# Attention maxima of a group placed by a table of ticks, on both sides of the value visits

## The reference

```
mod = silu(c) @ wmod                      # six parts of 1024 for each of the 4 batches
h = layernorm(x) * (1 + ca) + sa
q, k, v = h @ Wq, h @ Wk, h @ Wv          # 32 query heads, 8 key/value heads, 32 wide
q, k = rope(q), rope(k)
att = where(causal, q @ k.T / sqrt(32), -inf)
ctx = softmax(att) @ v                    # 1024 queries x 1024 keys for each head
x = x + ga * (ctx @ Wo)
h = layernorm(x) * (1 + cb) + sb
out = x + gb * (h @ W.T + bias + lora(h))
```

## Time and profile before

| | |
|---|---|
| median of three runs | 2497.97 us |
| the profiled execution | 2495.66 us, of it the span 2493.9 us |
| PE, DVE, ACT, POOL busy | 97%, 69%, 42%, 66% of the span |
| granted TensorE clock | 0.99 (mean) |
| last part of the chain, PE L1586 and L1539 | 14% and 13% of the span |

### The profile page before, as it was taken

The page is one execution under the profiler, slowest core; times in us unless marked ns, Lnnn a source line. Parts: engine busy times, 40 slices in busy tenths (PEclk is TensorE's granted clock), DMA queues, the critical chain, the costliest instruction groups (busy, mean ns, idle before and its releaser), DMA issues. The chain is left out here.

```text
span 2493.9 us, 36376 instructions
## 1 busy us (share of the span) xinstructions
PE 2406.7 (97%) x13140; PEld 1668.3 (67%) x13204; DVE 1723.4 (69%) x3392; ACT 1042.6 (42%) x1873; POOL 1650.8 (66%) x865
## 2 busy tenths in 40 slices
PE   5999999999999999999999999998999999999998
PEld 3788888887555555555555555544788788888886
DVE  4866666677888888888888888874555355455553
ACT  3433333231666666666666666665211111111111
POOL 3744333441799998999989999993655455545643
PEclk8999999999999999999999999999999999999999
DMA  6532333352545325344233345313333333323330
GB/s 236 198 118 87 115 113 118 123 150 80 162 100 146 82 64 154 83 132 97 71 79 83 83 117 132 84 31 127 112 92 101 103 90 97 118 86 104 107 93 25
DMA packets 179727, 267.45 MB, mean 107 GB/s; under 512 B 20508, under 2 KB 113884, under 8 KB 178400
## 3 DMA queue, kind: packets, MB, share of 16 engines
q1 hardware_dynamic: 179552, 265.13, 36.2%
HBM read 183.22 MB, written 80.81 MB: 106 GB/s over the span
## 5 line engine op out<-in xcount | busy, mean ns | idle before, releaser
L1082 POOL TENSOR_TENSOR p_sum<-p_sum,p_ring 128x1024 f32<-128x1024 f32 (+2 forms) x465 | 991.3, 2164 | 71.0 <-PE ctx_ps L1143 50.2
L976 ACT ACTIVATE p_ring<-scores 128x512 f32<-128x512 f32 (+1 forms) x896 | 448.9, 568 | 236.3 <-DVE scores L1030 173.6
L272 DVE TENSOR_REDUCE neg_max<-scores_q 128x1 f32<-128x512 f32 x679 | 438.8, 684 | 79.0 <-PE scores_q L253 64.9
L253 PE MATMUL scores_q<-k_stack,q_stack 96*128 96x512 f32 (+1 forms) x1473 | 443.0, 378 | 14.6 <-DVE neg_max L269 6.3
L1122 PE MATMUL scores<-q_stack,k_stack 98*128 98x512 f32 (+1 forms) x1216 | 409.7, 414 | 10.6 <-ACT p_ring L976 7.7
L253 PEld LDWEIGHTS scores_q<-k_stack,q_stack 96*128 96x128 f32 x1473 | 263.6, 191 | 135.4 <-DVE neg_max L269 64.5
L1122 PEld LDWEIGHTS scores<-q_stack,k_stack 98*128 98x128 f32 x1216 | 205.9, 190 | 184.7 <-ACT p_ring L976 71.9
L627 POOL TENSOR_TENSOR roped_hilo<-roped_hilo 128x512 fp32r<-128x512 f32 x80 | 105.5, 1319 | 337.0 <-ACT roped_hilo L467 337.0
L269 DVE CUSTOM_DVE_ANT_0 scores_q<-scores_q,masks 128x512 f32<-128x512 f32 x489 | 296.0, 642 | 38.4 <-PE scores_q L253 38.4
L676 PE MATMUL proj_ps<-h_hi,w_hi 128*128 128x512 f32 x752 | 298.7, 397 | 0.7 <-POOL w_lo L616 0.7
L676 PE MATMUL proj_ps<-h_hi,w_lo 128*128 128x512 f32 x752 | 294.1, 391 | 0.0
(11 more groups left out here) (182 smaller groups left out, 3632.8 us busy)
## 6 DMA issues: line engine op xcount, KB each, us to landing
q_stack<-qk_t SPq DMA_DIRECT2D x96, 512.0 KB, 6.8
qk_t<-roped_hilo SPq DMA_DIRECT2D x80, 512.0 KB, 2.8
x_in<-in_L_attn_resid SPq DMA_DIRECT2D x32, 512.0 KB, 6.3
ctx_t<-ctx_raw SPq DMA_DIRECT2D x64, 256.0 KB, 5.4
prefetched<-in_L_wmod SPq DMA_DIRECT2D x4, 4096.0 KB, 13.6
prefetched<-ctx_t SPq DMA_DIRECT2D x31, 512.0 KB, 4.0
prefetched<-inv_t SPq DMA_DIRECT2D x124, 128.0 KB, 5.5
k_stack<-qk_t SPq DMA_DIRECT2D x96, 128.0 KB, 8.8
```

Of the source, the lines that this page charges most:

```text
L253: last = nc.tensor.matmul(dst[:, a, :], qs[0:MHI, h, i * P:(i + 1) * P], ks[0:MHI, lo:lo + w], start=not first and (a == 0 or not diag), s ...
L272: nc.vector.tensor_reduce(neg, src, AX.X, ALU.max, negate=True).then_inc(sh.s_mx.sem, 1)
L976: nc.scalar.activation(p[:, a * per:(a + 1) * per, :], src[:, a * per:(a + 1) * per, :], ACT.Exp, scale=SM_SCALE).then_inc(s_ex.sem, 1)
L1082: nc.gpsimd.tensor_tensor(a, a, probs(n, u), ALU.add).then_inc(s_ap.sem, 1)
```

## The change

A number with ' is a unit of the group after the next. The code:

```diff
-BATCH = 2
-LAG = 2
-SUM_AT = {1: 9, 0: 16}
-AHEAD = 5
-TURN_AT = 17
-MAX_TICK = [m * NE // NM - AHEAD for m in range(NM)]
+AFTER = [
+    [],
+    maxima(1, 10, 11) + quads(-1, 10, 11) + maxima(1, 12),
+    maxima(1, 13),
+    ...
+    maxima(2, 6, 7, 8) + quads(0, 8, 9) + maxima(2, 9),
+]
+EARLY = [s[2] for r in AFTER for s in r if s[0] == "max" and s[1] == 2]
...
-        for at, t in ((n + 1, u), (n + 2, u - NE)):
-            if at < NG:
-                steps += [("max", at, m) for m in range(NM) if MAX_TICK[m] == t]
...
+        for step in AFTER[u]:
+            at = n + step[1]
+            if 0 <= at < NG and not (step[0] == "sum" and n >= NG - 1):
+                steps.append((step[0], at) + step[2:])
+        if n >= NG - 1:
+            for hf in range(2):
+                if u == SUM_AT_LAST[hf] and 0 <= n - hf < NG:
+                    steps.append(("sum", n - hf, hf))
...
-FIRST_MAXIMA = [(0, m) for m in range(NM)] + [(1, m) for m in range(NM) if MAX_TICK[m] < 0]
+FIRST_MAXIMA = [(0, m) for m in range(NM)] + [(1, m) for m in EARLY]
```

More of the change, by code:

```diff
@@ L99, with maxima, quads, sums_of @@
 QUARTER = D // 4
-MAX_TICK = [m * NE // NM - AHEAD for m in range(NM)]
+def maxima(ahead, *units):
+    return [("max", ahead, m) for m in units]
+def quads(ahead, *quads):
+    return [("values", ahead, q) for q in quads]
+def sums_of(ahead, hf):
+    return [("sum", ahead, hf)]
+def turned(ahead):
+    return [("turn", ahead)]
+AFTER = [
+    [],
+    maxima(1, 10, 11) + quads(-1, 10, 11) + maxima(1, 12),
+    maxima(1, 13),
+    maxima(1, 14, 15),
+    maxima(1, 16),
+    maxima(1, 17) + quads(0, 0, 1) + maxima(1, 18, 19),
+    [],
+    maxima(1, 20, 21, 22) + quads(0, 2, 3) + maxima(1, 23, 24),
+    maxima(1, 25),
+    maxima(1, 26) + sums_of(-1, 1) + maxima(1, 27),
+    [],
+    maxima(1, 28, 29, 30) + quads(0, 4, 5) + maxima(1, 31),
+    maxima(1, 32),
+    maxima(1, 33, 34),
+    maxima(1, 35, 36),
+    maxima(1, 37) + quads(0, 6, 7) + maxima(2, 0, 1),
+    maxima(2, 2) + sums_of(0, 0) + maxima(2, 3),
+    maxima(2, 4) + turned(1) + maxima(2, 5),
+    [],
+    maxima(2, 6, 7, 8) + quads(0, 8, 9) + maxima(2, 9),
+]
+EARLY = [s[2] for r in AFTER for s in r if s[0] == "max" and s[1] == 2]
 def group_steps(n):
@@ L129, in group_steps @@
                 steps.append(({MOD_AT: "mod", MOD_OUT: "mod_out", MOD_IN: "mod_in"}[u], i))
-        at, v = (n, u - LAG) if u >= LAG else (n - 1, u - LAG + NE)
-        if 0 <= at < NG and v == QUADS[QUAD_OF[v]][-1] and QUAD_OF[v] % BATCH == BATCH - 1:
-            steps += [("values", at, q) for q in range(QUAD_OF[v] - BATCH + 1, QUAD_OF[v] + 1)]
     return steps
 STEPS = [s for n in range(NG + 1) for s in group_steps(n)]
-FIRST_MAXIMA = [(0, m) for m in range(NM)] + [(1, m) for m in range(NM) if MAX_TICK[m] < 0]
+FIRST_MAXIMA = [(0, m) for m in range(NM)] + [(1, m) for m in EARLY]
 UNIT_AT = {}
```

## The result

| | before | after |
|---|---|---|
| median (four runs each) | 2497.69 us (2494.40 to 2500.48) | 2458.02 us (2457.52 to 2460.31) |
| ratio, with its 95% interval | 1 | 0.984 [0.983, 0.986] |
| profiled execution, of it the span | 2495.66, 2493.9 us | 2458.49, 2456.7 us |
| plain period of a group | 33.50 us | 31.89 us |

The change makes the kernel 39.7 us faster. The forecast was 2468, with a range of 2456 to 2496. The time lies inside the range, but within 1 us of the first rival, "POOL lags and costs nothing yet" (2459), and outside the forecast's own range of 2461 to 2476.

What follows compares the result with a forecast made beforehand. PE and DVE bound the kernel in turn; DVE's 28.80 us busy plus 3.4 idle made 32.2, so POOL's 32.47 would take over. Thirty periods by 1.0 us: 2497.97 - 30 = 2468 us, range 2456 to 2496.

Steps and rivals of the forecast that it cites:

- POOL lags and costs nothing yet: Rival, attention: POOL falls back 0.3 us a period within its 4.1 us margin, PE's pace counts; 2459 us, chance 0.13.
- The gain taken from DVE's idle times, piece by piece: Attention's plain period: DVE's six idle times shrink from 4.70 to 3.4 us, giving 32.2 us with 28.80 busy.
- POOL takes over, 32.5: Main case, plain groups: POOL's additions become the bound, period 32.5 us, 1.0 less; 2468 us, chance 0.50.
- the forecast's own sign, a period below 32.2: Test in the profile after: the forecast is wrong if the period is above 33.0 or below 32.2 us.
- Occupancy: Skill's rule, rival of no change: busiest engine POOL, 31.97 of 33.50 us, already bounds; 2498 us, chance 0.07.
- The wait of 1.03 us of POOL at tick 11 is gone: Sign at tick 11's visit: POOL's wait gone or below 0.1 us; if still there, POOL is not the bound.
- The turned rows: Turn's DMAs before tick 0's scores: most of the 0.5 us margin goes, costing 0 to 0.6 us, taken as 0.1.
- the slower rival: At the turn: its copy slips, DMAs land late, tick 0's scores wait; 0.3 us a period, 2507 us, chance 0.13.
- The sign that I had set, more than 0.62 us: Wait for the turned rows: if longer than 0.62 us and naming the DMA, the slower case came in part.
- Scores behind the visits cost nothing: Scores stand 0.23 us later behind six visits and two sums; ACT's idle time hides it, at most 1.8 us a period.
- Half of the gain (2483): Rival: ticks 6, 10 and 18 without maxima starve DVE; half the gain, 15 us, is left; chance 0.17.
- Groups with modulation: Attention groups with a piece of modulation, 36.74 us long, should lose the same 1.0 us as plain groups.

Runs made afterwards that it cites:

- after_relief: Changed kernel, with score unit 18's exponentials summed by PE instead of added by POOL, only in groups 25 to 30: 2444.92 us, ratio 0.979.
- after_tail6: Changed kernel, with score unit 18's exponentials summed by PE instead of added by POOL, in every group: 2463.07 us, ratio 0.986.
- before_tail6: Kernel before the change, with score unit 18's exponentials summed by PE instead of added by POOL, in every group: 2507.74 us, ratio 1.004.
- behind: Kernel before, two maxima per tick kept, but one of two moved directly behind each value visit, sum and turn: 2478.01 us, ratio 0.992.
- one_behind: Changed kernel, one unit moved from behind to in front of the visits at ticks 5 and 15: 2481.96 us, ratio 0.994.
- all_front: Changed kernel's counts per tick, but all maxima in front of the tick's visit, sum or turn: 2608.21 us, ratio 1.044.

## Why the prediction was right and where it was wrong

*The gain taken from DVE's idle times, piece by piece: right in kind, too small in size.* That busy and idle time together make the period is so for any engine; what was forecast is the pieces. Each, in us:

| piece | before | forecast | measured |
|---|---|---|---|
| behind the visit of tick 11 | 1.60 | 1.06 | 1.01 |
| behind the sum of tick 9 | 1.28 | 0.9 | 0.76 |
| ahead of unit 28, new | 0 | 0.5 | 0.48 |
| ticks 19 and 0 | 0.36 | 0.25 | 0.10 |
| tick 5 | 0.39 | 0 | 0.15 |
| ticks 7 and 8 | 0.47 | 0.23 | below 0.1 |
| ticks 15 to 17 | 0.50 | 0.45 | 0.25 |
| all | 4.70 | 3.4 | 2.8 |

The large ones, made from rows of loads, visits and reductions, are off by 0.14 at most. The small ones below them make 0.4 of the 0.6 by which the sum is off. DVE's busy time, forecast as unchanged, grew from 28.8 to 29.1. With the idle 2.8 that makes the period of 31.9 us; forecast was 32.2 from this sum.

*"POOL takes over, 32.5": wrong, and this is the step that failed.* By the forecast's own sign, a period below 32.2, it was wrong, though the time lies in the range. POOL does need 32.47 us for a group: its rows are 32.50 and 32.47 apart. But PE waits for it only once the margin is gone, and each modulation or inversion tops the margin up. I had priced just this as a rival and gave it 0.13. I had the numbers: at most four plain groups stand between two long ones and six behind the last, and by the forecast's own 0.3 a period that makes 1.8 us, less than 4.1. I let a comparison of two periods decide instead.

The rival's own sum was too easy as well. The changed order reaches the sum of tick 9 sooner, so the margin starts not at 4.1 us but at 2.9, and it shrinks by 0.6 a period and not 0.3. After four plain groups 0.6 us were left. Behind the last inversion it was 1.5 us, less than six plain groups use at 0.6 each, and POOL's two steps of 2.4 us for the next stage, which neither case had counted, took it sooner. PE's waits for POOL there are 11.5 us. `after_relief` shows these as real, `after_tail6` and `before_tail6` that nothing else of POOL is.

*That the time came within 1 us of the rival's 2459 is luck.* The 1.57 instead of 1.3 us in each of 25 periods, and 4.7 us of the last stage, most of them by its clock, helped. The waits for POOL at the end, the three periods in which the clock fell, and 1.8 us ahead of the first copy went the other way.

*Occupancy.* The rule of the Trainium skill (Perfetto Trace Analysis, section Identifying the Most-Contended Engine) would have named POOL, and no change. `before_tail6` decides: POOL at 95% was made lighter by 2.4 us a group, and the kernel became slower by 0.4%. The measurement decides against the rule here. My forecast had weighed it, and then took POOL as the bound all the same, only one step later.

*The wait of 1.03 us of POOL at tick 11 is gone:* right; POOL's rows show nothing above 0.17 us in the period. But this sign does not tell the two cases apart: a POOL that only lags loses the wait too.

*The turned rows:* the slower rival did not come, but its mechanism did in small. The margin of 0.5 us is gone, and PE waits about 0.2 us a period for the rows, where I took 0.1. The sign that I had set, more than 0.62 us, was no measure, as the 0.62 belongs to the visit and not to the DMA.

*Scores behind the visits cost nothing:* right within what shows; in a plain period no pause of PE that names ACT is longer than 0.36 us.

*Half of the gain (2483) did not come, but the reason I gave for the gain was half of it.* I counted what DVE gets sooner behind a visit. `behind` shows 0.77 of the 1.61 us with the counts of before: from units no longer held up for a bank in front of a visit, one behind it each time. That these waits are the cause is read from the trace and not tried by itself. The other 0.84 us come only with the uneven table, and `one_behind` gives 0.91 back by one unit moved ahead at each of the visits of ticks 5 and 15. Emptied ticks without these two behind bring 0.05. So the parts seem to depend on each other, which the forecast did not have. It is not fully shown: two units behind these two visits without the emptied ticks were not run.

*Groups with modulation* were to gain the same 1.0 us as the plain ones. They went from 36.7 to 37.5 us down to 35.3 to 35.9, 1.4 to 1.6 less, near the 1.6 of a plain group: right that they gain the same, wrong in the size. The groups with an inversion were not looked at apart. One of three gained 1.4 us; in the other two the granted clock fell to 0.95 over the period and took the gain away. "No part of the change is about the clock" holds for the plain period and not for these.

Open: why the clock fell behind a pause in some groups and not behind the same pause in others; how the 0.9 us of the two units splits between ticks 5 and 15, and between a unit more in front and a unit less behind; and how much of the 13 us of `after_relief` is the edit in the runs without a profile.

## What to carry to other kernels

Where an in-order engine feeds another through a few banks and has a long job between, put fillers on both sides of it: enough in front to keep the reader busy, none that waits for a bank, and one or two behind (more were not tried). Test a busy engine as a bound by its queue: the margin at the place that waits for it, divided by what it falls back each period, is the number of periods for which it costs nothing. Take both as they will be in the changed kernel, and count the engine's odd steps too. A wait that names a DMA is one only if the DMA landed last: hold its landing against the end of the wait. An engine that only lags is relieved where the margin ends, since relief in every period is paid for in every period.

## What was unexpected in the hardware

In `all_front` the granted clock fell behind a pause of PE of 1.41 us. Its PEld, ahead of a visit, and then the same place in a later group:

```profile
1011.82 0.19 PEld L282 LDWEIGHTS scores_q<-k_stack,q_stack 96*128 96x128 f32 x1 [1.41 <-DVE neg_max L298]
1012.41 0.20 PEld L1172 LDWEIGHTS ctx_ps<-p_ring,v 128*32 128x32 f32 x8 [0.41 <-ACT p_ring L1001]
1013.27 0.20 PEld L1172 LDWEIGHTS ctx_ps<-p_ring,v 128*32 128x32 f32 x4 [0.66 <-issue]
...
1159.20 0.19 PEld L282 LDWEIGHTS scores_q<-k_stack,q_stack 96*128 96x128 f32 x1 [1.41 <-DVE neg_max L298]
1159.63 0.16 PEld L1172 LDWEIGHTS ctx_ps<-p_ring,v 128*32 128x32 f32 x8 [0.24 <-ACT p_ring L1001]
1160.09 0.13 PEld L1172 LDWEIGHTS ctx_ps<-p_ring,v 128*32 128x32 f32 x4 [0.30 <-issue]
```

```profile
1008.00:1012.00 4.00, 3.00 (x12) 1.72 (x12) 3.50 (x12) 2.93 (x7) 4.00 (x2) 1.00 0.03 8
1012.00:1016.00 4.00, 4.00 (x19) 1.05 (x20) 1.71 (x6) 0.25 (x1) 4.00 (x3) 0.58 0.84 188
```

In the first, the loads of the visit come 0.86 us apart, in the second 0.46: the visit ran at about half the clock. The second block is two windows around the first pause. The granted clock of the 4 us behind it was 0.58, most of it at the lower level (1.2 GHz), and back at 1.00 in the next 4 us. Groups with the fall have a period of 37.7, those without 36.05: 1.6 us each. The same pause stands in all of them, so a pause of this length is not enough by itself. The Trainium skill (TensorE: Matmul & The Clock Gate, section A second HAM failure mode: psum-queue depth-cycling) tells of a kernel that idles briefly between its groups of matmuls as it goes through PSUM banks, and whose clock goes back and forth between its levels by that. This trace agrees as far as a clock that falls behind a short pause and comes back, 0.58 and then 1.00; that the changes of bank are the reason it doesn't show.

The kernel after has it too. In the periods with an inversion PE pauses 1.83, 1.75 and 1.75 us for DVE (PEld at 910.08, 1175.07 and 1437.64). Behind the first two the clock fell, behind the third it did not. The windows of 4 us behind the second and the third:

```profile
1176.00:1180.00 4.00, 4.00 (x21) 0.91 (x19) 2.88 (x11) 2.17 (x4) 4.00 (x3) 0.57 0.00 0
1438.00:1442.00 4.00, 4.00 (x30) 2.08 (x29) 3.86 (x15) 2.17 (x4) 4.00 (x2) 1.00 0.08 27
```

It fell as well behind the wait of 2.34 us for POOL, in the 27th period, and not behind that of 2.00 in the 29th. In the kernel before the longest pause in these places is 1.66 us, and the clock stayed at 1.00. In the plain periods of after, with pauses of up to 0.84 us, it stayed at 1.00.
